# One loop of sixteen four-row groups in place of twelve five-row groups with two small groups behind them

## What is computed

```python
keep = (u >= 0.1).astype(x.dtype)
x_drop = x * keep / (1.0 - 0.1)
y = x + jnp.matmul(adj, x_drop)
m = jnp.mean(y, axis=-1, keepdims=True)
v = jnp.var(y, axis=-1, keepdims=True)
out = (y - m) / jnp.sqrt(v + 1e-05)
```

## Time and profile before

| | |
|---|---|
| median of 3 runs | 643.25 us (643.08 to 644.87) |
| the profiled execution's own time | 643.32 us |
| its span, first to last instruction | 641.4 us |
| TensorE (matmul) busy | 509.1 us, 79% |
| VectorE busy | 60.7 us, 9% |
| ScalarE busy | 17.0 us, 3% |
| read from and written to memory | 272.63 MB and 2.10 MB, 428 GB/s over the span |
| mean granted TensorE clock | 0.907 |

### The profile page before, as it was taken

How to read it: one execution, slowest core, us unless ns; L and a number is a source line. 1 busy time by engine, 2 the same in 40 slices (tenths; PEclk the granted TensorE clock), 3 DMA queues, 4 the chain that set the end, 5 groups by cost and what they waited for, 6 DMA issues and landing times.

```text
span 641.4 us, 7694 instructions
## 1 busy us (share of the span) xinstructions
PE 509.1 (79%) x3458; PEld 264.0 (41%) x3458; DVE 60.7 (9%) x268; ACT 17.0 (3%) x24; POOL 1.1 (0%) x8
## 2 busy tenths in 40 slices
PE   0098798797898688788888887987778878979897
PEld 0044344343444344444443443443434434435446
DVE  1200100100100100100100100010100010010202
ACT  0000000000000000000000000000000000000000
POOL 0000000000000000000000000000000000000000
PEclk9998988987979978978978987989978978979999
DMA  9999999999999999999999999999999999999997
GB/s 384 429 430 446 426 429 450 429 429 450 429 429 450 429 429 419 460 429 396 437 444 423 433 429 442 429 433 446 429 429 450 429 429 450 429 410 426 424 423 321
DMA packets 7348, 274.80 MB, mean 428 GB/s; under 512 B 944, under 2 KB 1072, under 8 KB 1456
## 3 DMA queue, kind: packets, MB, share of 16 engines
q1 hardware_dynamic: 7200, 274.70, 99.3%
q10 hardware_dynamic: 144, 0.03, 0.0%
HBM read 272.63 MB, written 2.10 MB: 428 GB/s over the span
## 4 chain that ended last, share of the span: by engine, by line
DMA 65%; PE 34%; issue 0%; DVE 0%; SPq 0%; ACT 0%; ACTq 0%; DVEq 0%
DMA adj_ring<-adj_blocks 65%; PE acc L234 29%; PE tail_acc L234 5%; PE back L241 0%; SPq L151 0%; PE final L272 0%; SPq L153 0%; DVE x_and_u L341 0%; ACT std L224 0%; DVE acc_sb L279 0%; ACTq L202 0%; DVE stats L335 0%; PE final L269 0%; DVE mean_var L337 0%; DVE rstd L339 0%
## 5 line engine op out<-in xcount | busy, mean ns | idle before, releaser
L234 PE MATMUL acc<-adj_ring,x_and_u 128*64 128x320 f32 x3072 | 462.0, 466 | 114.6 <-ACTq L202 114.6
L234 PEld LDWEIGHTS acc<-adj_ring,x_and_u 128*64 128x64 f32 x3072 | 231.7, 148 | 339.7 <-ACTq L202 122.7
L279 DVE COPY acc_sb<-acc 128x320 f32<-128x320 f32 x24 | 10.7, 485 | 472.9 <-PE acc L234 472.9
L234 PE MATMUL tail_acc<-adj_ring,x_and_u 128*64 128x384 f32 (+1 forms) x256 | 29.8, 395 | 2.0 <-DMA adj_ring<-adj_blocks 2.0
L241 PE MATMUL back<-twofold,acc_sb 128*128 128x64 f32 x126 | 16.8, 280 | 11.9 <-DVE acc_sb L279 11.9
L196 ACT ACT_TABLE_LOAD x10 | 12.8, 1283 | 502.5 <-DMA adj_ring<-adj_blocks 502.5
L234 PEld LDWEIGHTS tail_acc<-adj_ring,x_and_u 128*64 128x64 f32 x256 | 16.7, 141 | 14.8 <-issue 12.5
L241 PEld LDWEIGHTS back<-twofold,acc_sb 128*128 128x128 f32 x126 | 15.0, 191 | 18.8 <-DVE acc_sb L279 18.6
L310 DVE TENSOR_SCALAR x_and_u<-summed,mean,rstd 128x64 f32 (+1 forms) x63 | 15.2, 309 | 0.5
L288 DVE BATCH_NORM_STATS2 stats<-summed 128x6 f32<-128x64 f32 x63 | 9.3, 213 | 0.4
L284 DVE TENSOR_TENSOR summed<-back,x_and_u 128x320 f32<-128x320 f32 (+1 forms) x13 | 6.3, 481 | 20.9 <-PE back L241 20.9
(11 more groups left out here) (17 smaller groups left out, 3.9 us busy)
## 6 DMA issues: line engine op xcount, KB each, us to landing
adj_ring<-adj_blocks SPq DMA_DIRECT2D x23, 7680.0 KB, 33.3
adj_ring<-adj_blocks SPq DMA_DIRECT2D x11, 5120.0 KB, 36.9
adj_ring<-adj_blocks SPq DMA_DIRECT2D x1, 6400.0 KB, 30.4
adj_ring<-adj_blocks SPq DMA_DIRECT2D x1, 4608.0 KB, 25.8
x_and_u<-xu SPq DMA_DIRECT2D x1, 4096.0 KB, 12.2
adj_ring<-adj_blocks SPq DMA_DIRECT2D x1, 3840.0 KB, 30.9
adj_ring<-adj_blocks SPq DMA_DIRECT2D x1, 3072.0 KB, 32.8
adj_ring<-adj_blocks SPq DMA_DIRECT2D x1, 2560.0 KB, 36.7
```

What stands on the lines that cost most here:

```text
L234: return nc.tensor.matmul(into[h * D:(h + 1) * D, 0:cols], x_drop[:, t * D:(t + 1) * D], adj_ring[:, at:at + cols], start=(t < 2), stop=(t ...
L279: last = nc.vector.tensor_copy(acc_sb[:, b * cols:(b + 1) * cols], part[:, 0:cols])
```

## The change

All 64 rows now go through the one loop, in 16 turns of R = 4 rows. The ring is 128 KB in each partition, a slot of 24 tiles is 6144 KB (was 7680) and one of 16 tiles 4096 KB (was 5120). A turn's 512 columns are one PSUM tile and one matmul for each k tile. The last turn arrives in seven loads of 24, 14, 10, 8, 4, 2 and 2 k tiles, and its four rows go through `take`, `turn_back` and `normalise` like any other turn's. SyncE stores the first 60 rows once the fifteenth turn is normalised, ScalarE the last four. The diff (the deletion of declarations cut):

```diff
-R = 5
-FULL = 12
+R = 4
+FULL = 16
 TILE = R * P
 SLOT_TILES = [24, 24, 16]
...
-LAST_TILES = [24, 20, 12, 8]
+LAST_TILES = [24, 14, 10, 8, 4, 2, 2]
...
-COLS = TILE // 2
+COLS = TILE
 SPLIT = TILE // COLS
-
-TAIL = [(3, [24, 16, 10, 8, 6]), (1, [20, 18, 14, 8, 4])]
-LAST = len(TAIL) - 1
...
@@ sync
-            for n in range(len(TAIL)):
-                for i, (_, _, at, width) in enumerate(pieces(n)):
-
-                    slot = sum(at + width > first * TILE for first in SLOT_FIRST)
-                    sp.wait_ge(adj_used, MAIN - SLOTS + slot)
-                    sp.dma_start(adj_ring[:, at:at + width], block_of(FULL, at, width)).then_inc(piece_loaded[n][i], 16)
-
-            sp.wait_ge(normed_ready, FULL)
-            cols = slice(0, FULL * R * D)
-            sp.dma_start(out_rows[:, cols], normed[:, cols]).then_inc(out_stored, 16)
-            sp.wait_ge(normed_ready, FULL + LAST)
-            cols = slice(FULL * R * D, (KT - 1) * D)
+
+            sp.wait_ge(normed_ready, FULL - 1)
+            cols = slice(0, (FULL - 1) * R * D)
             sp.dma_start(out_rows[:, cols], normed[:, cols]).then_inc(out_stored, 16)
@@ scalar
             root(FULL - 1, R)
-            for n in range(LAST):
-                root(FULL + n, TAIL[n][0])
-            act.wait_ge(final_var, 1)
-            nc.scalar.activation(std[:, 0:1], mean_var[:, 1:2], ACT.Sqrt, bias=eps[:]).then_inc(std_ready, 1)
-            act.wait_ge(normed_ready, FULL + LAST + 1)
-            cols = slice((KT - 1) * D, KT * D)
+            act.wait_ge(normed_ready, FULL)
+            cols = slice((FULL - 1) * R * D, KT * D)
             act.dma_start(out_rows[:, cols], normed[:, cols]).then_inc(out_stored, 16)
-            act.wait_ge(out_stored, 16 * 3)
+            act.wait_ge(out_stored, 16 * 2)
@@ tensor
                 turn_back(R, g)
-
-            for n, (rows, _) in enumerate(TAIL):
-                for i, (before, count, at, _) in enumerate(pieces(n)):
-                    pe.wait_ge(piece_loaded[n][i], 16)
-                    for t in range(before, before + count):
-                        col = at + (t - before) * rows * P
-                        last = product(tail_acc[n], rows * P, col, t)
-                    last.then_inc(adj_used, 1)
-                    if n == LAST and i == 0:
-
-                        turn_back(TAIL[n - 1][0], FULL + n - 1)
-                        nc.tensor.matmul(final[:, 0:D], identity[:], x_nat[:, (KT - 1) * D:KT * D],
-                                         start=True, stop=False)
-            pe.wait_ge(acc_copied, FULL + LAST + 1)
-            nc.tensor.matmul(final[:, 0:D], acc_sb[:, 0:P], twofold[:], start=False, stop=True).then_inc(final_ready, 1)
@@ vector
             with dve.Fori(0, FULL) as g:
                 take(acc, COLS, (g + 1) * SLOTS)
                 normalise(g, g * R, R)
-            for n in range(LAST):
-                rows = TAIL[n][0]
-                take([tail_acc[n]], rows * P, MAIN + FIRST_PIECE[n] + len(TAIL[n][1]))
-                normalise(FULL + n, FIRST_ROW[n], rows)
-
-            take([tail_acc[LAST]], P, MAIN + FIRST_PIECE[LAST] + len(TAIL[LAST][1]))
...
```

More of the change, by code:

```diff
@@ L28 @@
 RING = KT * TILE
-COLS = TILE // 2
+COLS = TILE
 SPLIT = TILE // COLS
-TAIL = [(3, [24, 16, 10, 8, 6]), (1, [20, 18, 14, 8, 4])]
-LAST = len(TAIL) - 1
-FIRST_ROW = [FULL * R + sum(rows for rows, _ in TAIL[:n]) for n in range(len(TAIL))]
-FIRST_PIECE = [sum(len(tiles) for _, tiles in TAIL[:n]) for n in range(len(TAIL))]
 X_PARTS = 4
@@ L40 @@
 PT = KT // X_PARTS
[L42 to L54, removed]
+assert FULL * R == KT and sum(SLOT_TILES) == sum(LAST_TILES) == KT
 def build(nc: bass.Bass, xu: bass.AP, adj: bass.AP, out: bass.AP):
@@ L106, in build @@
         rstd = sb("rstd", [P, R])
-        mean_var = sb("mean_var", [P, 2])
         acc = [ps(f"acc{b}", 512) for b in range(SPLIT)]
-        tail_acc = [ps(f"tail_acc{n}", 512) for n in range(len(TAIL))]
         back = ps("back", 512)
-        final = ps("final", 512)
         x_loaded = sem("x_loaded")
@@ L118, in build @@
         tiles_ready = sem("tiles_ready")
-        piece_loaded = [[sem(f"piece_loaded{n}_{i}") for i in range(len(tiles))]
-                        for n, (_, tiles) in enumerate(TAIL)]
         adj_used = sem("adj_used")
@@ L139, in build @@
         normed_ready = sem("normed_ready")
-        final_ready = sem("final_ready")
-        final_stats = sem("final_stats")
-        final_var = sem("final_var")
         out_stored = sem("out_stored")
@@ L364 @@
             put((g * RING + before * TILE) * P, g * R, R, before, count)
-    for n, (rows, _) in enumerate(TAIL):
-        for before, count, at, _ in pieces(n):
-            put((FULL * RING + at) * P, FIRST_ROW[n], rows, before, count)
     x_and_u = np.concatenate([x.reshape(P, KT * D), u.reshape(P, KT * D)], axis=1)
```

## The result

The changed kernel takes 649.51 us (median of 4 runs, 649.14 to 650.15), the kernel before, beside it, 643.16 us: 1.0101 times as long, with a 95% interval of 1.0089 to 1.0113. The forecast was 648.7 us, in a range of 646.0 to 651.0. The span of the profiled execution is 647.8 us for 641.4.

A forecast was written before the change was run, and what follows sets the result against it. The load stream at 433 GB/s bounds the body, TensorE the end. TensorE's end 639.4 + 0.1 + finish 5.2 = 644.7, + 1.9 + 0.2 = 646.8 span, + 1.9 around it = 648.7 us; range 646.0 to 651.0.

The forecast's parts named there:

- The loop costs nothing but the stream's change: Sixteen four-row turns: TensorE needs 36 to 39 us a turn, at or just below the stream's 38.7, so no cost.
- the slow clock: TensorE's last turn: 1.8 us lost to a lowered granted clock after an idle time of 2 to 3 us.
- The number of loads: Load stream: five more loads of `adj` at 0.05 us each, +0.3 us on E (bounds 0 and +0.5).
- E: The time the last load lands: 634.7 us in the kernel before, forecast 634.5 after the change.
- Code fetches: Load stream: fewer instruction packets holding it up, taken as -0.5 us on E (bounds 0 and -1.6).
- Rival 2: Not slower: all four code packets cost 3.2 us in all and go; with Rival 1, 644.2 us; 7%.
- TensorE's end: Last turn: first piece lands at 609.9, 29.5 us of work follows, ending at 639.4, +2.2 us against before.
- Rival 1: Last turn: the clock stays up, TensorE ends 1.8 us earlier, 646.9 us; 15%.
- The finish: After TensorE's end: four rows finished together take 5.20 us against 2.16 for one row, +3.05 us.
- The stores: End of kernel: 60-row store over by about 638, before VectorE is done; last store 1.7 us for 1.5.
- The table load: ScalarE's load in the loop's body, fourteen times: nothing, unless one stands before the last root (bound 0 to +1.3 us).
- Rivals 3 and 4: 3: five loads pay 1.5 us each, 656 us, 2%; 4: 32 KB pitch halves slot rate, +145 us, 2%.

The follow-up runs named there:

- the loop alone: Kernel before with its loop changed to 15 turns of four rows, its three-row and one-row tail kept: 644.17 us, ratio 1.0019.
- the end alone: Kernel before with its five-row loop kept and one four-row group behind it, finished together: 649.7 us, ratio 1.0098.

## Why the prediction was right, point by point

- **The loop costs nothing but the stream's change.** Right in kind: the period is 38.78 us for the 38.7 forecast, and TensorE waits in every turn. Too low in size: the loop alone costs 1.1 us, some 0.7 of it by nine more loads and the rest by the slow clock at its end. One step in it was wrong: I had three waits a turn, each with a slow stretch behind it, and so 36 to 39 us of need. Only each turn's first slot has the slow stretch; the 80 records behind it take 17.39 us from the second turn on, the time at full clock, and TensorE's need is some 32 us. The margin before a slot's space is needed again, some 12 us in the forecast, is 11.2 at the end (space free at 584.97, the transfer ahead in the queue done at 596.19).
- **The number of loads.** +0.3 us at 0.05 each. Measured 0.065 to 0.09 each, so 0.3 to 0.45. The loads that I counted from the landing at 565.17 to E are 13 and not 14, which hardly moves the price.
- **Code fetches.** The term that failed. I took -0.5 us from E because three packets would go. They did go, and nothing came of it: the stream lost 1.55 us in its first turn before and after. In the first turn after, the 24-tile slots land 42.11 - 27.57 = 14.54 us apart, and the 16-tile slot comes 53.36 - 42.11 = 11.25 later, where two thirds of 14.54 is 9.7. The late slot moved to where the packet is (it was the second slot before), its cost stayed. Rival 2 rested on these packets and falls with them.
- **TensorE's end.** First piece forecast for 609.9, seen at 610.8. E was 635.2 for 634.5 (the last load is issued at 605.3 and lands after 29.9 us): 0.5 of these 0.7 us is the code term, the rest lies within the price of the loads. The first piece landed at 610.7, 24.5 us ahead of E for the 24.6 forecast, and TensorE took it up 0.1 us after. The work from there: 29.5 forecast, 29.44 seen; end 639.4 forecast, 640.25 seen. That the first piece sets the end, and not the last bytes, was shown from both sides, by coarse last pieces (0.4 to 0.8 us longer, not the 2.6 of that rival) and a small first piece (2.7 us back).
- **The slow clock** of 1.8 us in the last turn was measured alone: 29.44 less 27.64. Rival 1, the clock that stays up, didn't happen: the idle time was 4.96 us, not the 2 to 3 that I reckoned with, as the turn ahead ran its last 80 records at full clock. So there is luck in the 1.8 us. My ground against rival 1, that every wait of 2 us and more is followed by the slow stretch, doesn't hold: five waits of 2.12 to 2.58 us ahead of the 80 records of a turn of the changed kernel are followed by full clock, and so is the 2.28 us of the small first piece. (The 2.0 us of before came right behind `turn_back` and the wait ahead of it.) Had the idle time been the 2 to 3 us that I reckoned with, the term might have been nothing.
- **The finish.** 5.20 forecast, 5.25 seen; copy 0.69 and 0.69.
- **The stores.** 1.7 forecast, 1.8 seen; the 60-row store was over at 639.8 for 638, still before VectorE's end. **The table load** came fourteen times and, as before, not ahead of the last root.
- **Rivals 3 and 4** (loads that cost by themselves, a pitch of 32 KB) fell: a queued load costs 0.065 to 0.09 us, and the 16-tile slots keep the stream's pace, with a period of 0.80 of the old one.

The sum was 0.8 us short, 649.5 for 648.7, and that is the first piece's time, above all the code term. The packets that went had cost the stream nothing that can be seen, and the one that goes with 1.55 us stayed.

## What to carry to other kernels

Where a kernel lives from one long stream of loads, look at when the last group's first piece lands and how much work waits for it: if that work is longer than the stream has left, the size of the first piece and the number of rows in the group set the end, and cutting the last pieces smaller buys nothing. The last group should be small in rows as well, since what follows the product (copy, transposition, statistics, scaling) is paid in full after the last product, 5.25 us for four rows and 2.16 for one, which here has a shorter way of its own too. Merging small groups into the main loop makes a simpler program, but here these two terms were its price, and each can be read from the timeline of the kernel before.

## What the runs showed that I had not expected

- The slow clock after the same idle time doesn't cost the same each time. In the changed kernel each turn's first slot follows 4.96 us of idle time, and takes 13.46, 12.88 or, in other turns, as little as 11.94 us, where 10.52 is its time at full clock: 1.4 to 2.9 us lost. From turn to turn the loss drops by 0.6 us and then jumps back by 1.1:

```profile
416.93 11.94 PE L194 MATMUL acc<-adj_ring,x_and_u 128*64 128x512 f32 x48 [4.97 <-ACTq L166]
...
455.69 13.03 PE L194 MATMUL acc<-adj_ring,x_and_u 128*64 128x512 f32 x48 [4.96 <-ACTq L166]
...
494.48 12.42 PE L194 MATMUL acc<-adj_ring,x_and_u 128*64 128x512 f32 x48 [4.96 <-ACTq L166]
```

  So what a wait of TensorE costs near the end depends on when it falls (and shorter waits, as said above, cost no clock at all), and two kernels that differ elsewhere may differ by some 0.8 us for that alone (29.44 and 30.28 us for the same 128 records in the changed kernel and in the end alone).
- Matmuls of 64 columns of weights that all write the same half of the partitions take 0.44 us for a record of 512 columns; those that alternate between the halves take 0.22 (8.37 us for 19 against 4.51 for 20).
- In all twelve profiles the first 16 KB code packet goes with one slot that lands 1.1 to 1.6 us late, the slot that is in transfer when the packet comes (between 41 and 53 us); a second one some 20 us later does nothing. Why the first costs more than the second is open.
